# An expert loop over turns of four tiles, written out on three engines

## The chip, the cores and the metric

The kernel runs on one core of one Trainium2 chip. The metric is device time in microseconds (us), the median of several executions; a profiled execution of the same program gives the trace. Five engines work side by side, each with its own stream of instructions and its own sequencer: PE (TensorE, matrix products), ACT (ScalarE), DVE (VectorE), POOL (GpSimd) and SP (SyncE, which here only issues DMAs). They meet only through semaphores.

## The reference, cut to what matters

One layer over 32 x 64 tokens of width 256: attention over itself and over a context, and behind it a mixture of experts with a dense shared branch. The part around the change is the routed one:

```python
E, TOPK, INTER = 8, 2, 512
logits = x @ router_w
top_logits, top_indices = jax.lax.top_k(logits, TOPK)
scores = jax.nn.softmax(top_logits, axis=-1)
sorted_pos = jnp.argsort(top_indices.reshape(-1), stable=True)
permuted = x[sorted_pos // TOPK]
expert_ids = top_indices.reshape(-1)[sorted_pos]
for e in range(E):
    mask = (expert_ids == e)[:, None]
    g, u = jnp.split(permuted * mask @ w1[e], 2, axis=-1)
    out = out + jnp.where(mask, silu(g) * u @ w2[e], 0.0)
# each token: its two rows, weighted by its scores, plus the shared branch
```

## The kernel before

Everything is on one core and in one program: first the attention (up to about 690 us), then the shared branch with the routing beside it, and from about 813 us the routed experts, in a block of its own. Only that last block is touched.

The routed rows, 2 x 2048 of them, were sorted by expert and scattered to a buffer in HBM, each expert's rows padded to whole tiles of 128. There are ET = 39 tiles (line 42). A tile belongs to one expert, which is known only when the kernel runs. The weights of all eight experts lie in SBUF as two 16-bit parts each (`w1h`, `w1l`, `w2h`, `w2l`), so that an expert's weights are read at an address that a register holds.

The tiles are taken in turns of TURN = 4 (line 43). For each turn one word of `ecode` holds the numbers of six experts as digits to the base 8: those of its own four tiles and of the two after. `experts(q, count)` (line 1611 on) reads that word on PE with a value load (line 1613) and splits it into registers (line 1617). This stands at the head of each turn.

One slot, for tile t, holds on PE, in this order (`turn`, line 1621 on):

- `first(t + 2)`: 12 products of the gate and up projection into `b_eg` and `b_eu` (line 1588), which wait for `gl` of that tile from DVE and for the `ea` of the tile before
- `gather_T(t + 3)`: 4 transposes of the tile's rows into `b_x` (line 1578)
- `second(t)`: 12 products of the down projection into `b_ey` (line 1606)
- `product_T(t + 1)`: 8 transposes of the activation into `b_a` (line 1598)

ACT and DVE have slots of their own, in step with this: ACT `gate` (line 1654, `esg`), `high` (line 1650, `gh`), `split` (line 1660, `eah`), `output` (line 1669, into the tile's own row in `xg`) and `high_T` (line 1665, `aTh`); DVE `product` (line 1707, `ea`), `low` (lines 1700 and 1701, `gl` and `uys`), `split` (line 1712, `eal`) and `low_T` (line 1717, `aTl`). The two parts of a number, high and low, make the products exact enough in 16 bits.

POOL adds each finished tile to `out` in HBM with an indirect DMA that accumulates (line 1567); it waits for ACT's `output` of that tile and for the landing of the DMA before it. POOL's 39 steps are written out already. SP loads the tiles of the later turns in eight DMAs in a loop of its own (line 1554 on) and one more behind it.

ET = 39 gives NQT = 9 whole turns and a rest of three tiles. Turn 0 is written out, since its rows lie in another tile (`xhl`). Turns 1 to 8 are one body in a hardware loop, in which `t` is computed from the loop's register: on PE in line 1641, on ACT and DVE in `slots` (line 1535 on, the loop in line 1539). The rest is written out again.

Of the kernel before, what the change touches and what calls it, by code (L numbers as in the profile page):

```python
# [41 lines left out]
ET = (2 * T + E * (P - 1)) // P  # L42
TURN = 4
# [22 lines left out]
def build(nc, x, ctxT, cols, w_all, wprojT,  # L66
# [4 lines left out]
    with ExitStack() as top:  # L71
# [69 lines left out]
        def after(eng, name, count):  # L141

            if not (isinstance(count, int) and count <= 0):
                eng.wait_ge(s[name], count)
# [919 lines left out]
        with ExitStack() as ph:  # L1064
# [94 lines left out]
            @block.sync  # L1159
            def _(sp):  # L1160
                attention_sync(sp)
                sp.wait_ge(s["proj_done"], 4 * (4 * NT - 2))
                for n in range(NPC):
                    if n == 2:
                        sp.wait_ge(s["wsq_done"], NPC)
                    after(sp, "wl_done", n - 2)
                    sp.dma_start(stage[n % 3][:, :], ffw[n, :, :]).then_inc(s[f"wst_in{n % 3}"], 16)
                    if n == 4:
                        store_rows(sp, NT - 2)
                    if n == 6:  # L1170
                        store_rows(sp, NT - 1)
                        sp.wait_ge(s["row_out"], 16 * NT)
                        sp.wait_ge(s["proj_done"], 16 * NT)
                        sp.dma_start(xn[:, :, 0:2 * H].bitcast(U32), rowbuf).then_inc(s["rows_in"], 16)
                sp.wait_ge(s["scattered"], 16 * 2 * NT)
                sp.wait_ge(s["gu_done"], NS)
                sp.dma_start(xg0.bitcast(U32), x_rows[:, 0:TURN, :])\
                    .then_inc(s["xg_in"], 16)
                sp.wait_ge(s["xg_in"], 16)
# [335 lines left out]
        with ExitStack() as ph:  # L1515
            NQT = ET // TURN
# [19 lines left out]
            def slots(eng, slot):  # L1536
                for t in range(TURN):
                    slot(t, t % 2)
                with eng.Fori(1, NQT) as q:
                    for n in range(TURN):  # L1540
                        slot(TURN * q + n, n % 2)
                for t in range(NQT * TURN, ET):
                    slot(t, t % 2)

            def xrow(t):
                return row(xg0, t) if isinstance(t, int) and t < TURN else row(xg, t - TURN)

            def exists(t):
                return not isinstance(t, int) or t < ET
# [21 lines left out]
            @block.tensor  # L1571
            def _(pe):
                def gather_T(t, n, m):
                    if m == 0:
                        pe.wait_ge(s["xg_in"], 16 * (t // TURN + 1) if isinstance(t, int) else 16 // TURN * t + 16)
                    after(pe, "gl_done", t)
                    for k in range(2 * KT):
                        last = pe.transpose(b_x[:, 0, k * P:(k + 1) * P], xrow(t)[:, k * P:(k + 1) * P], ident16[:, :])  # L1578
                    last.then_inc(s["gT_done"], 1)

                def first(t, n, e):
                    pe.wait_ge(s["gl_done"], t + 1)
                    after(pe, "ea_done", t - 1)
                    for k in range(KT):
                        for m, (xx, w) in enumerate(((gh, w1h), (gh, w1l), (gl, w1h))):
                            for c, o in enumerate((b_g[n], b_u[n])):
                                at = k * 2 * F + c * F
                                last = pe.matmul(o[:, :], xx[n][:, k * P:(k + 1) * P],  # L1588
                                                 w[:, bass.ds(e, 1), at:at + F].rearrange("p a b -> p (a b)"),
                                                 start=(k == 0 and m == 0), stop=(k == KT - 1 and m == 2))  # L1590
                    last.then_inc(s["eh_done"], 1)

                def product_T(t, n):
                    pe.wait_ge(s["eal_done"], t + 1)
                    after(pe, "aTl_done", t)
                    for m, a in enumerate((ah, al)):
                        for c in range(FK):
                            last = pe.transpose(b_a[:, m, c * P:(c + 1) * P], a[n][:, c * P:(c + 1) * P], ident16[:, :])  # L1598
                    last.then_inc(s["aT_done"], 1)

                def second(t, n, e):
                    pe.wait_ge(s["aTl_done"], t + 1)
                    after(pe, "ysb_done", t)
                    for c in range(FK):
                        for m, (a, w) in enumerate(((aTh, w2h), (aTh, w2l), (aTl, w2h))):
                            last = pe.matmul(b_y[:, 0:H], a[n][:, c * P:(c + 1) * P],  # L1606
                                             w[:, bass.ds(e, 1), c * H:(c + 1) * H].rearrange("p a b -> p (a b)"),
                                             start=(c == 0 and m == 0), stop=(c == FK - 1 and m == 2))
                    last.then_inc(s["ey_done"], 1)

                def experts(q, count):

                    code = pe.value_load(ecode[0:1, bass.ds(q, 1)], min_val=0, max_val=E ** CODE - 1)
                    held = []
                    for n in range(count):
                        reg = pe.alloc_register()
                        pe.reg_mov(reg, code // E ** n % E)
                        held.append(bass.RuntimeValue.of_register_unchecked(reg, min_val=0, max_val=E - 1))
                    return held

                def turn(q, t0, slots):
                    es = experts(q, min(slots + 2, ET - t0) if isinstance(t0, int) else CODE)
                    for n in range(slots):
                        t = t0 + n
                        if exists(t + 2) and exists(t + 3):
                            first(t + 2, n % 2, es[n + 2])
                            gather_T(t + 3, (n + 1) % 2, (n + 3) % TURN)
                        second(t, n % 2, es[n])
                        if exists(t + 1):
                            product_T(t + 1, (n + 1) % 2)  # L1630
                        if exists(t + 2) and not exists(t + 3):
                            first(t + 2, n % 2, es[n + 2])

                for t in range(3):
                    gather_T(t, t % 2, t)
                es = experts(0, 2)
                first(0, 0, es[0])
                first(1, 1, es[1])
                product_T(0, 0)
                turn(0, 0, TURN)  # L1640
                with pe.Fori(1, NQT) as q:
                    turn(q, TURN * q, TURN)
                turn(NQT, NQT * TURN, REST)

            @block.scalar
            def _(act):
# [34 lines left out]
                def slot(t, n):  # L1681
# [7 lines left out]
                    if exists(t + 2) and not exists(t + 3):  # L1689
                        gate(t + 2, n)  # L1690
                        split(t + 2, n)

                slots(act, slot)

            @block.vector
# [98 lines left out]
```

## Time and profile before

| | |
|---|---|
| median of 3 runs | 1024.51 us (1024.0 to 1026.1) |
| the profiled execution | 1024.13 us |
| its span in the trace | 1022.0 us |
| mean granted clock of PE over the span | 0.986 of full speed |
| PE busy | 955.7 us, 94% of the span |
| DVE busy | 797.4 us, 78% |
| ACT busy | 735.2 us, 72% |
| POOL busy | 452.4 us, 44% |
| the routed stage, turns 1 to 8 on PE | 841.44 to about 1000 us |

All times in the trace are counted from the span's start. The span is what the engines' records cover; the time of the execution is a little longer. PEld is PE's loading of weights, which runs beside its products.
### The profile page before, as it was taken

The numbers are of one execution on the slowest core, as the hardware profiler recorded it, in microseconds if no ns is written. First come the engines' busy times: TensorE is split into PE (matmuls) and PEld (weight loads), VectorE is DVE, ScalarE is ACT, GpSimd is POOL, SyncE is SP. The second block draws the span as 40 slices with busy tenths as digits, with TensorE's granted clock in tenths as the row PEclk, the third lists the DMA queues.
The fourth block names the chain that finished last, engine by engine and source line by source line (L and its number), as shares of the span: only waits on it lengthen the run. The fifth ranks groups of instructions, "written<-read, shape, count | busy, mean of one in ns | idle before, by whom it ended". The sixth has DMA issues, their size and how long they took to land. (4 is left out here: it accounts for less than half of the span.)

```text
span 1022.0 us, 22255 instructions
## 1 busy us (share of the span) xinstructions
PE 955.7 (94%) x7240; PEld 677.0 (66%) x7241; DVE 797.4 (78%) x1704; ACT 735.2 (72%) x1364; POOL 452.4 (44%) x673
## 2 busy tenths in 40 slices
PE   5588999999999999999999999989999799999994
PEld 3356677777777777777777777756556456666663
DVE  7678999999999999999999999886997444444441
ACT  6868898898898898898898898753655354454552
POOL 5224556455455455455455455501066113333332
PEclk9899999999999999999999999999999999999997
DMA  9923311011011011001011011315266553222222
GB/s 266 252 77 63 62 36 34 27 34 36 27 34 35 28 32 38 27 31 38 27 32 37 28 31 38 109 47 171 86 207 191 185 147 69 26 30 27 26 26 26
DMA packets 37100, 70.16 MB, mean 69 GB/s; under 512 B 3984, under 2 KB 25104, under 8 KB 36880
## 3 DMA queue, kind: packets, MB, share of 16 engines
q1 hardware_dynamic: 27552, 54.39, 17.3%
q0 software_dynamic: 9456, 14.59, 8.4%
q8 instruction: 52, 0.85, 0.3%
q14 instruction: 40, 0.33, 0.1%
HBM read 55.52 MB, written 18.68 MB: 73 GB/s over the span
## 5 line engine op out<-in xcount | busy, mean ns | idle before, releaser
L664 POOL TENSOR_TENSOR root<-vareps,neghalf 128x4 f32<-128x4 f32 (+1 forms) x128 | 174.4, 1362 | 10.0
L657 POOL TENSOR_TENSOR var<-ssq,unit 128x4 f32<-128x4 f32 (+1 forms) x128 | 53.1, 415 | 252.0 <-DVE ssq L496 252.0
L329 PE MATMUL b_pj<-w_hi,xq 128*128 128x512 f16 x384 | 147.7, 385 | 1.8 <-DVE xq L647 1.5
L329 PE MATMUL b_pj<-w_lo,xq 128*128 128x512 f16 x384 | 146.9, 382 | 0.0
L430 ACT ACTIVATE sq<-b_pj 128x512 f32<-128x512 f32 x192 | 114.3, 595 | 44.2 <-PE b_pj L329 41.5
L496 DVE TENSOR_REDUCE ssq<-sq 128x4 f32<-128x512 f32 x192 | 130.1, 677 | 11.9 <-ACT sq L430 11.9
L507 DVE TENSOR_TENSOR nrm<-raw,rstd 128x512 f32<-128x512 f32 x192 | 128.1, 668 | 1.1 <-POOL rstd L668 0.8
L355 PEld LDWEIGHTS b_sc<-kT,qT 128*128 128x128 f32 x1024 | 122.4, 192 | 5.0 <-ACT qT L456 0.3
L355 PE MATMUL b_sc<-kT,qT 128*128 128x64 f32 x1024 | 122.8, 273 | 0.0
L345 PE MATMUL b_tr<-ident,nrm 128*128 128x128 f32 x768 | 117.1, 275 | 5.3 <-DVE nrm L507 5.1
L440 ACT ACTIVATE raw<-b_pj 128x512 f32<-128x512 f32 x192 | 115.8, 603 | 0.0
L345 PEld LDWEIGHTS b_tr<-ident,nrm 128*128 128x128 f32 x768 | 94.0, 146 | 31.7 <-DVE nrm L507 8.0
L1567 POOL DMA_INDIRECT out<-xg x35 | 54.3, 1551 | 114.9 <-ACT xg L1669 90.8
L456 ACT ACTIVATE qT<-b_tr,col 128x512 f32<-128x512 f32 x128 | 99.8, 780 | 4.0 <-PE b_tr L345 4.0
L1707 DVE SCALAR_TENSOR_TENSOR ea<-b_eu,uu,esg 128x512 f32<-128x512 f32 x39 | 29.3, 751 | 88.6 <-ACT esg L1654 88.6
L545 DVE TENSOR_TENSOR cat<-b_o,rsm 128x512 bf16<-128x512 f32 x128 | 81.8, 680 | 4.2 <-PE b_o L382 4.2
L1654 ACT ACTIVATE esg<-b_eg,ug 128x512 f32<-128x512 f32 x39 | 26.8, 687 | 74.8 <-PE b_eu L1588 74.8
L382 PE MATMUL b_o<-probT,v 64*128 64x128 f32 x1024 | 74.4, 285 | 0.0
L382 PEld LDWEIGHTS b_o<-probT,v 64*128 64x128 f32 x1024 | 62.1, 187 | 11.5 <-issue 11.5
L456 ACT ACTIVATE kT<-b_tr,col 128x512 f32<-128x512 f32 x64 | 49.5, 773 | 25.0 <-PE b_tr L345 25.0
L419 PE MATMUL b_acc<-wproj,catq 128*128 128x256 f16 x512 | 66.3, 272 | 0.0
L329 PEld LDWEIGHTS b_pj<-w_hi,xq 128*128 128x128 f16 x384 | 37.7, 98 | 33.1 <-DVE xq L647 1.8
(312 smaller groups left out, 2316.3 us busy)
## 6 DMA issues: line engine op xcount, KB each, us to landing
nst<-in_ffw SPq DMA_DIRECT2D x40, 512.0 KB, 3.6
wload<-in_ffw SPq DMA_DIRECT2D x20, 512.0 KB, 3.9
xbuf<-zero SPq DMA_DIRECT2D x39, 129.0 KB, 4.0
xg<-xbuf SPq DMA_DIRECT2D x8, 516.0 KB
x_sb<-in_x SPq DMA_DIRECT2D x4, 512.0 KB, 13.0
wproj<-in_ctxT SPq DMA_DIRECT2D x1, 2048.0 KB, 9.7
xhl<-in_w_all SPq DMA_DIRECT2D x4, 512.0 KB, 20.3
wproj<-in_wprojT POOLq DMA_DIRECT2D x4, 512.0 KB, 6.1
```

Source lines behind the costliest of these rows:

```text
L329: last = pe.matmul(o, x, w[kind][:, k, at:at + BANK], start=(k == 0 and n_ == 0), stop=(k == KT - 1 and n_ == len(terms) - 1))
L345: last = pe.transpose(o, nrm[:, c, hd * P:(hd + 1) * P], ident[:, :])
L355: last = pe.matmul(b_sc[:, (g * 2 + b) * S:(g * 2 + b + 1) * S], qT[:, r % 2, g * 2 + b, :], kT[:, r % 2, g, b * S:(b + 1) * S], start=Tru ...
L382: last = pe.matmul(b_o[b][:, g * P:(g + 1) * P], v[b * S:(b + 1) * S, r, g, :], probT[b * S:(b + 1) * S, r % 2, g, :], start=True, stop=True)
L419: last = pe.matmul(b_acc[:, 0:H], catq[:, r % 2, hd, :], wproj[:, r * n + hd, :], start=(r == 0 and hd == 0), stop=(r == 3 and hd == n - 1))
L430: act.activation(sq[:, (r * NN + c) % 2, :], b_pj[c % 2][:, :], ACT.Square).then_inc(s["sq_done"], 1)
L440: act.activation(raw[:, r % 2, c, :], bk, ACT.Copy).then_inc(s["raw_done"], 1)
L456: act.activation(flat(dst), b_tr[:, :], ACT.Identity, scale=col[:, at:at + 1], bias=col[:, at + 1:at + 2]).then_inc(s["tev_done"], 1)
L496: dve.tensor_reduce(ssq[:, r % 2, c, :], sq[:, (r * NN + c) % 2, :].rearrange("p (a b) -> p a b", b=D), axis=AX.X, op=ALU.add).then_inc(s[ ...
L507: dve.tensor_tensor(nrm[:, c, :].rearrange("p (a b) -> p a b", b=D), raw[:, r % 2, c, :].rearrange("p (a b) -> p a b", b=D), wide(rstd[:, ...
L545: last = dve.tensor_tensor(cat16[:, :, b * S:(b + 1) * S], b_o[b][:, :].rearrange("p (a b) -> p a b", b=S), wide(rsm[:, r * n:(r + 1) * n] ...
L664: pool.tensor_tensor(root[:, r % 2, c, :], vareps[:, r % 2, c, :], neghalf[:, 0:1].unsqueeze(2).to_broadcast(shape), ALU.pow).then_inc(s[" ...
```

## The change

The hardware loop over turns 1 to 8 is replaced by a loop of the program's builder, which writes the eight bodies out one after the other. This is done for PE and, in `slots`, for ACT and DVE. The work, its order on each engine and the waits between engines stay. `t` and `q` are then constants: addresses and the values waited for are too, apart from the expert's number, which is read as before from `ecode` at the head of each turn. SP's loop and POOL's stream are left as they are.

```diff
@@ -1536,10 +1536,7 @@
             def slots(eng, slot):
                 for t in range(TURN):
                     slot(t, t % 2)
-                with eng.Fori(1, NQT) as q:
-                    for n in range(TURN):
-                        slot(TURN * q + n, n % 2)
-                for t in range(NQT * TURN, ET):
+                for t in range(TURN, ET):
                     slot(t, t % 2)
 
             def xrow(t):
@@ -1638,7 +1635,7 @@
                 first(1, 1, es[1])
                 product_T(0, 0)
                 turn(0, 0, TURN)
-                with pe.Fori(1, NQT) as q:
+                for q in range(1, NQT):
                     turn(q, TURN * q, TURN)
                 turn(NQT, NQT * TURN, REST)
```

## Rows read from the trace of the kernel before

**Rows 1.** Page, part 2: PE's busy share in 40 slices of the span, in tenths

```profile
PE   5588999999999999999999999989999799999994
```

**Rows 2.** Waits, 790 to 1022 us: who waited for whom, us in total, times, longest

```profile
PE b_eg L1588 <- issue: 6.2, 9, 1.5
...
PE b_eg L1588 <- DVE gl L1700: 1.4, 8, 0.2
```

**Rows 3.** Timeline of PE, a slot's first product: start, duration, idle before in brackets

```profile
831.80 0.39 PE L1588 MATMUL b_eg<-w1h,gh 128*128 x1
...
836.41 0.39 PE L1588 MATMUL b_eg<-w1h,gh 128*128 x1
...
841.44 0.39 PE L1588 MATMUL b_eg<-w1h,gh 128*128 x1 [0.28 <-issue]
...
871.10 0.39 PE L1588 MATMUL b_eg<-w1h,gh 128*128 x1
...
875.89 0.39 PE L1588 MATMUL b_eg<-w1h,gh 128*128 x1
...
980.62 0.39 PE L1588 MATMUL b_eg<-w1h,gh 128*128 x1 [0.60 <-issue]
...
995.13 0.39 PE L1588 MATMUL b_eg<-w1h,gh 128*128 x1
```

**Rows 4.** Timeline of all engines, a slot of turn 0, written out

```profile
834.19 0.38 PE L1588 MATMUL b_eu<-w1h,gl 128*128 x1
834.60 0.69 ACT L1654 ACTIVATE esg<-b_eg,ug 128x512 f32<-128x512 f32 x1 [1.62 <-PE b_eu L1588]
...
835.32 0.75 DVE L1707 SCALAR_TENSOR_TENSOR ea<-b_eu,uu,esg 128x512 f32<-128x512 f32 x1 [1.89 <-ACT esg L1654]
835.99 0.28 DVE L1700 COPY gl<-b_x 128x256 f16<-128x256 f16 x1
```

**Rows 5.** The same in the loop; last, ACT's register operation, from line 1654's instructions

```profile
873.48 0.38 PE L1588 MATMUL b_eu<-w1h,gl 128*128 x1
874.00 0.69 ACT L1654 ACTIVATE esg<-b_eg,ug 128x512 f32<-128x512 f32 x1 [1.72 <-PE b_eu L1588]
...
874.80 0.75 DVE L1707 SCALAR_TENSOR_TENSOR ea<-b_eu,uu,esg 128x512 f32<-128x512 f32 x1 [2.08 <-ACT esg L1654]
875.47 0.28 DVE L1700 COPY gl<-b_x 128x256 f16<-128x256 f16 x1
...
L1654 ACTq FUSED_REGOPS  x1: 43/43/43, 873.9 to 873.9; - x1
```

**Rows 6.** Instructions of lines 1641, 1613: ns min/median/max, first and last start us

```profile
L1641 PEldq COMPARE_BRANCH  x8: 79/218/245, 859.1 to 998.3; - x8
L1641 PEldq MOVE  x1: 37/37/37, 839.5 to 839.5; - x1
...
L1613 PEldq TENSOR_LOAD <-ecode x1: 315/315/315, 839.7 to 839.7; - x1
```

**Rows 7.** Timeline of ACT (the output of tile 4), then of POOL's scatters

```profile
846.70 0.46 ACT L1669 ACTIVATE xg<-b_ey,uys 128x256 f32 x1
...
850.18 1.55 POOL L1567 DMA_INDIRECT out<-xg  x1 [3.24 <-DMA out<-xhl]
...
881.92 1.55 POOL L1567 DMA_INDIRECT out<-xg  x1 [3.09 <-ACT xg L1669]
...
1000.89 1.56 POOL L1567 DMA_INDIRECT out<-xg  x1 [3.23 <-ACT xg L1669]
...
1010.09 1.55 POOL L1567 DMA_INDIRECT out<-xg  x1 [3.08 <-DMA out<-xg]
...
1014.57 1.55 POOL L1567 DMA_INDIRECT out<-xg  x1 [2.93 <-ACT xg L1669]
```

**Rows 8.** DMA queue of instruction fetches, 100 to 700 and 815 to 850 us: packets, MB, share

```profile
q8 instruction: 39, 0.64, 0.4%
...
q8 instruction: 3, 0.05, 0.6%
```

## Prediction, made before the changed kernel was seen

> **What bounds the kernel now.** I read the page first: PE is busy for 94% of the span, and at nine tenths or more in most of its 40 slices [rows 1], so only idle time of PE, or what makes PE late, is worth anything. The change touches only the routed stage, from about 813 us to the end. There I read who waited for whom [rows 2]: PE stands idle ahead of the first gate product `b_eg` for two reasons, 6.2 us in 9 places named "issue" (PE's own sequencer is not ready) and 1.4 us in 8 places on DVE's `gl`. These sums miss short gaps, because a matmul record is longer than the distance to the next. So the view to trust is the timeline: the starts of the first `b_eg` product of each slot [rows 3]. A slot that is written out (turn 0) lasts 836.41 - 831.80 = 4.61 us. The same slot inside the loop lasts 875.89 - 871.10 = 4.79 us, with the same 36 matmuls. The loop thus costs 0.18 us in every slot, besides what the turn's edge costs.
>
> **Where the 0.18 us comes from.** I follow the one ring that runs through three engines: last product of `first` on PE, then `gate` on ACT, `product` and `low` on DVE, then the next `first` on PE. Written out [rows 4, 3]: 834.19 to 834.60 (0.41), to 835.32 (0.72), to 835.99 (0.67), to the next `b_eg` at 836.41 (0.42), 2.22 us. In the loop [rows 5, 3]: 873.48 to 874.00 (0.52), to 874.80 (0.80), to 875.47 (0.67), to 875.89 (0.42), 2.41 us. The two links that are longer are those in which ACT and DVE must compute an address between the wait and the operation: ACT's register operation of 43 ns with its gap [rows 5] costs 0.10 us, DVE's likewise 0.09 us. Written out, `t` is a constant and neither exists. PE is then at its own pace, since in turn 0 the last transpose and the next `first` are almost back to back.
>
> **The change part by part, against the profiled execution's own time (span 1022.0 us, 1024.13 us with what lies around it).**
>
> 1. The loop's own instructions on PE. A back edge has an addition, a branch (218 ns median) and one register operation before the code is loaded [rows 6]; with their gaps that is about 0.50 us (0.03 + 0.22 + 0.05 and three gaps of 0.06, the gap being what MOVE at 839.5 and the load at 839.7 leave beside 37 and 50 ns). There are seven taken branches, one entry (about 0.20 us) and one exit. The head of each turn stays: value load, the range check and the digits. It can't be hidden, since `first` needs its digits and PE's queue runs dry.
>
> 2. What a written-out turn will last. The slot from 836.41 to 841.44 is the nearest row [rows 3]: its four stages are written out, and at its end stands a head with the entry's 0.20 us in it. Less that, a slot with a head is 5.03 - 0.20 = 4.83 us. A turn is then 3 x 4.61 + 4.83 = 18.66 us. Before, seven turns from head to head lasted 980.62 - 841.44 = 139.18 us, 19.88 each.
>
> 3. The sum on PE. At the first head 0.20. Over the seven turns 139.18 - 7 x 18.66 = 8.56. The last three slots of the loop, from 980.62 to 995.13 [rows 3], are 14.51 us and become 13.83: 0.68. Behind the loop the path goes once more through ACT and DVE before PE can go on, which gives another 0.19 by the links above; the exit branch lies beside that and gives nothing. Sum 9.6 us. The last tile would be ready that much earlier, and its scatter could start at 1014.57 - 9.6 = 1005.0 [rows 7], where it is released by ACT.
>
> 4. What is late next: POOL. It adds one tile at a time to `out` and waits for each landing before the next issue. At tile 4 it is behind: ACT has written that tile by 846.70 + 0.46, but its scatter starts only at 850.18, released by the DMA before it [rows 7]. That start hangs on landings that are slow while the big loads run, and none of them moves. From there seven cycles bound by landings last 881.92 - 850.18 = 31.74 us, and two more near the end 1010.09 - 1000.89 = 9.20: mean 4.55 us. Now the slots are longer (19.88 / 4 = 4.97 us) and POOL catches up by tile 11. After the change they average 18.66 / 4 = 4.67, only 0.12 us more than POOL's cycle, so its lag of some 3 us takes about 26 tiles to close. Scatter-bound all the way, tile 38 would start at 850.18 + 34 x 4.55 = 1004.9. So both chains arrive within 0.1 us of each other, and the end follows the later of the two, each with its own scatter. I add 0.2 us for that: 1005.2, a gain of 9.4 us. Nothing waits for POOL but the end, since the rows of `xg` are not used again.
>
> 5. Code that is written out must be fetched. Queue q8 moves it in packets of 16 KB. The trace can't show what a fetch costs in turns 1 to 8, for there the loop fetches none. In the attention stage 39 packets came in 600 us, and their time is 0.4% of 16 engines, 0.98 us each [rows 8], while PE was at nine tenths or more in each of those slices [rows 1]. In the written-out part of the routed stage 3 packets came in 35 us [rows 8], and the slots of 4.61 us are timed in just that part. At this rate the new turns need some 12 more. The bounds are 0 (all ahead of need) and 12 x 0.98 = 11.8 us (PE waits for each in full). I take 0, by the nearest row, which is the same code written out.
>
> The Trainium skill, "Runtime: NRT & Kernel Launch", section "Instruction fetch mechanics", says that crossing a 16 KiB block is mostly hidden and that a taken branch to a page no longer held stalls. The second would make the back edge dearer than I reckon; here it does not show, as the branches took 0.08 to 0.25 us [rows 6]. The first agrees with turn 0.
>
> 6. ACT's and DVE's own loop instructions go too. They lie beside PE's work except for the two links counted above: nothing more. SP's loop of loads is not touched.
>
> **The rivals.**
>
> - The scatter chain is slower than its mean. It is bound by landings at every tile, and other traffic (the fetches among it) may lengthen each. Against it: nine cycles average 4.55. With 4.64 throughout, tile 38 starts at 850.18 + 34 x 4.64 = 1007.9, a gain of 6.7: 1017.8 us. This takes over as soon as a cycle exceeds 4.56.
> - Only the branches are saved, and the 0.18 us per slot stays (because, say, the addresses of the routed expert, which stay in registers, set the slot). For it: PE keeps its register operations for the weights. Against it: turn 0 has these too and runs at 4.61. Then 7 x 0.50 + 0.20, and 0.2 for the exit, 3.9 us: 1020.6 us.
> - The other side: PE waits for its code. Mechanism: each of 12 new 16 KB packets on q8 arrives late. Price up to 0.98 us each; 11.8 us against 9.4 gained is 2.4 us slower, 1026.9 us. It decides from 9.4 / 12 = 0.78 us per packet. Against it: turn 0 and the attention stage. Half that stall would give 1021.
> - The change doesn't reach the chip's time, because the instructions that remain refill the space: no change, 1024.5 us.
>
> **How the numbers follow.** The median of the runs is 1024.51, 0.38 above the profiled execution. Forecast: 1024.13 - 9.4 + 0.4 = 1015.1 us. Chances: forecast as summed, 0.66; slower scatter chain, 0.14; only the branches, 0.07; some stalls for code but still a gain, 0.04; PE waits for its code and the kernel is slower, 0.06; no change, 0.03. The range takes in the first two: the low end is the sum with every head at its shortest and POOL always in time (9.6 and 0.1 less at each of eight heads, 10.4), 1014.1, put at 1014.0; the high end is the slow scatter chain, 1018.0. That holds 0.80. A measurement of this kernel can tell about 0.2% (2 us) from no change; so faster 0.91, within 0.03, slower 0.06.
>
> **What would show it.** Right: every slot without a head at 4.61 us from one `b_eg` to the next, slots with a head at 4.83; no branch and no register operation of ACT or DVE between turns; idle time on `gl` gone while "issue" before `b_eg` stays, smaller; POOL released by its own DMA up to the last third of the stage, at 4.5 to 4.6 us per tile; about 12 more packets on q8. Wrong: slots of 4.79 (second rival), idle time of PE in places that are no heads (third), or a last scatter that starts later than 1006 and is released by a DMA (first).

## The result, and the profile after

| | before | after |
|---|---|---|
| median | 1024.26 us (4 runs, 1023.8 to 1026.1) | 1015.91 us (4 runs, 1014.6 to 1016.7) |
| the profiled execution | 1024.13 | 1016.18 |
| its span | 1022.0 | 1014.5 |
| first `b_eg` of turn 0's last slot (tile 5) | 836.41 | 838.11 |
| first `b_eg` of tile 37 | 995.13 | 987.33 |
| start of the last scatter | 1014.57 | 1007.05 |
| instructions in the trace | 22255 | 21771 |

The ratio of the times is 0.9914, with a 95% interval from 0.9897 to 0.9931: 8.4 us faster by the medians, where 9.4 was forecast. Measured twice more beside before, the same kernel gave 0.9936 (0.991 to 0.9962) and 0.9926 (0.9911 to 0.994).

First the waits in the profile after, 790 to 1015 us (who waited for whom, us in total, times, longest):

```profile
POOL out L1564 <- DMA out<-xg: 74.8, 24, 4.1
...
POOL out L1564 <- ACT xg L1666: 30.1, 10, 3.1
...
PE b_eg L1585 <- issue: 1.5, 2, 1.3
```

Against [rows 2], PE's idle time named "issue" ahead of `b_eg` fell from 6.2 to 1.5 us, and the line on `gl` is gone. The view names POOL's own DMA 24 times; the same row of before, at the tiles in `xg`, was

```profile
POOL out L1567 <- DMA out<-xg: 20.9, 7, 3.1
```

The timeline of PE after, at the starts of slots (the first product of `first`; line 1585 is 1588 of before):

```profile
838.11 0.39 PE L1585 MATMUL b_eg<-w1h,gh 128*128 x1
...
842.90 0.39 PE L1585 MATMUL b_eg<-w1h,gh 128*128 x1
...
861.52 0.39 PE L1585 MATMUL b_eg<-w1h,gh 128*128 x1
...
866.13 0.39 PE L1585 MATMUL b_eg<-w1h,gh 128*128 x1
...
870.74 0.39 PE L1585 MATMUL b_eg<-w1h,gh 128*128 x1
...
987.33 0.39 PE L1585 MATMUL b_eg<-w1h,gh 128*128 x1
```

The slot after a head is now 866.13 - 861.52 = 4.61 us, a plain one the same, and one with a head 842.90 - 838.11 = 4.79, against 4.79 and 5.03 in [rows 3]. The ring that [rows 5] showed in the loop, from the trace after:

```profile
868.51 0.38 PE L1585 MATMUL b_eu<-w1h,gl 128*128 x1
868.93 0.69 ACT L1651 ACTIVATE esg<-b_eg,ug 128x512 f32<-128x512 f32 x1 [1.63 <-PE b_eu L1585]
...
869.65 0.75 DVE L1704 SCALAR_TENSOR_TENSOR ea<-b_eu,uu,esg 128x512 f32<-128x512 f32 x1 [1.89 <-ACT esg L1651]
870.32 0.28 DVE L1697 COPY gl<-b_x 128x256 f16<-128x256 f16 x1
```

Its links are 0.42, 0.72 and 0.67 us, and 0.42 to PE at 870.74: those of [rows 4] within a hundredth. At POOL (timeline, with the output of the last tile on ACT put last):

```profile
849.44 1.55 POOL L1564 DMA_INDIRECT out<-xg  x1 [3.00 <-DMA out<-xhl]
...
886.14 1.55 POOL L1564 DMA_INDIRECT out<-xg  x1 [2.99 <-ACT xg L1666]
891.72 1.55 POOL L1564 DMA_INDIRECT out<-xg  x1 [4.03 <-DMA out<-xg]
...
1007.05 1.55 POOL L1564 DMA_INDIRECT out<-xg  x1 [2.97 <-ACT xg L1666]
...
1005.90 0.47 ACT L1666 ACTIVATE xg<-b_ey,uys 128x256 f32<-128x256 f32 x1 [3.38 <-PE b_ey L1603]
```

The last scatter starts 1007.05 - 1005.90 = 1.15 us behind the start of ACT's output. Where a scatter waits for ACT alone that distance is 0.73 to 0.75 us; at the last tile of before it was 0.80. So some 0.35 us of the gain went to the landings.

The names in the waits hide how tight this chain is. In the profile after, every one of the 34 scatters from tile 5 to 38 starts 0.77 us after the landing of the one before, also the ten that the view puts down to ACT: POOL never caught up. In before only ten of the 34 do so, tiles 5 to 11 and the last three. Tiles 36 and 37 are bound by landings in every trace with all scatters, and tile 38 in all but pe_alone and act_dve, since ACT's output of tile 36 comes only 3.1 us behind that of tile 35.

Queue q8 moved 11 packets of code from 850 to 990 us:

```profile
q8 instruction: 11, 0.18, 0.6%
```

### The profile page after: what moved, and what is told of

The parts are those of the page before. It is cut to its first block and busy times, and to the rows that moved or that the text cites. A ratio compares the mean times of both kernels' runs of the same rounds, so it can differ in the third digit from the quotient of the medians.

```text
span 1014.5 us, 21771 instructions
## 1 busy us (share of the span) xinstructions
PE 952.3 (94%) x7240; PEld 676.3 (67%) x7240; DVE 797.7 (79%) x1704; ACT 735.2 (72%) x1364; POOL 448.5 (44%) x673
```

## The experiments

Absolute times differ between executions by a microsecond or two before the changed code is reached, so two distances within a trace are compared: from the first `b_eg` of turn 0's last slot to that of tile 37 (PE's pace), and from the same point to the last scatter. A "slot with a head" is the one at whose end the turn's code is read.

| kernel | time, us (runs), beside before | to tile 37 | to last scatter | slots: plain (median), after a head, with a head |
|---|---|---|---|---|
| before | 1024.3 to 1025.5, medians | 158.72 | 178.16 | 4.80, 4.92, 5.29 to 5.52 |
| after | 1015.91 (4), 1024.26 | 149.22 | 168.94 | 4.61, 4.61, 4.78 to 4.99 |
| after2 | 1016.99 (5), 1025.50 | 149.38 | 168.65 | 4.61, 4.61, 4.82 to 4.88 |
| after3 | 1016.05 (6), 1024.82 | 149.42 | 168.83 | 4.61, 4.61, 4.78 to 5.04 |
| pe_alone | 1022.39 (10), 1025.50 | 155.63 | 175.06 | 4.80, 4.92, 4.80 to 5.07 |
| act_dve | 1019.30 (4), 1025.50 | 153.00 | 172.24 | 4.61, 4.61, 5.08 to 5.38 |
| act_alone | 1022.94 (1), 1024.74 | 156.07 | 175.47 | 4.70, 4.81, 5.02 to 5.39 |
| dve_alone | 1021.22 (1), 1024.74 | 155.45 | 174.76 | 4.71, 4.72, 5.11 to 5.39 |
| few_scatters | 1015.33 (1), 1024.74 | 151.16 | 170.40 | 4.61, 4.61, 4.86 to 5.14 |
| pe_few | 1020.64 (1), 1024.74 | 154.67 | 174.74 | 4.80, 4.92, 4.80 to 4.81 |
| early_codes | 1013.96 (4), 1025.50 | 147.64 | 167.73 | 4.61, 4.61, 4.61 |
| early_codes2 | 1014.51 (4), 1024.82 | 147.59 | 172.10 | 4.61, 4.61, 4.61 |
| early_few | 1010.90 (1), 1024.82 | 147.52 | 166.75 | 4.61, 4.61, 4.61 to 4.65 |
| loop_early | 1013.45 (4), 1024.86 | 148.65 | 168.02 | 4.61, 4.61, 4.74 to 4.76 |

### Which engine's loop costs what

`pe_alone` undoes the change on ACT and DVE, `act_dve` undoes it on PE:

```diff
# pe_alone, against before
-                with pe.Fori(1, NQT) as q:
+                for q in range(1, NQT):
# act_dve, against after
-                for q in range(1, NQT):
+                with pe.Fori(1, NQT) as q:
```

> Only PE's turns are written out; ACT and DVE keep their loop. Theory (the slot is set by the ring through ACT and DVE, the head by PE): slots in the loop's part stay at 4.80 us, the one after a head at 4.92, slots with a head fall from 5.3 to about 4.83; 7 x 0.5 + 0.2 + 0.2 = 3.9 us less than before: about 1020.4 us. Rival (PE's own register operations for addresses and waits set the slot): slots fall to 4.61, and the time to that of the changed kernel, 1015 to 1016 us.

> Only ACT and DVE are written out; PE keeps its loop. Theory: slots fall to 4.61 us, also the one after a head; slots with a head stay at about 5.3; per turn 19.88 becomes 13.83 + 5.32 = 19.15, so 7 x 0.73 + 0.68 + 0.19 = 6.0 us less: about 1018.3 us. With the run in which PE alone is written out the two gains add up to 9.6 to 9.9. Rival (PE's register operations): slots stay at 4.79 and nothing is gained, 1024 us.

Timelines of PE in pe_alone:

```profile
866.59 0.39 PE L1588 MATMUL b_eg<-w1h,gh 128*128 x1 [0.18 <-DVE gl L1700]
871.39 0.39 PE L1588 MATMUL b_eg<-w1h,gh 128*128 x1
...
876.19 0.39 PE L1588 MATMUL b_eg<-w1h,gh 128*128 x1
...
881.26 0.39 PE L1588 MATMUL b_eg<-w1h,gh 128*128 x1 [0.29 <-issue]
```

and in act_dve:

```profile
870.13 0.39 PE L1585 MATMUL b_eg<-w1h,gh 128*128 x1
...
874.74 0.39 PE L1585 MATMUL b_eg<-w1h,gh 128*128 x1
...
880.04 0.39 PE L1585 MATMUL b_eg<-w1h,gh 128*128 x1 [0.55 <-issue]
```

Written out on PE alone, the plain slot stays at 4.80 us and the idle time on `gl` stays. Written out on ACT and DVE alone it is 4.61, while PE still runs its loop. So the rival that put the 0.18 us on PE's own register operations is out. The distance to tile 37 falls by 3.09 and 5.72 us; together 8.81, where the whole change gives 9.50. By the medians the two gave 3.1 and 6.2 us, where 3.9 and 6.0 were expected. Most of what pe_alone lacks shows in its slots with a head: some are 4.80 us, four are 5.04 to 5.07, a matter that comes up again below.

`act_alone` and `dve_alone` give `slots` a second form and use it on one engine:

```diff
-            def slots(eng, slot):
+            def slots(eng, slot, written=False):
+                if written:
+                    for t in range(ET):
+                        slot(t, t % 2)
+                    return
...
-                slots(act, slot)
+                slots(act, slot, True)
```

(for `dve_alone` the last line is that of DVE).

> Only ACT's turns are written out; PE and DVE keep the loop. Theory (each link of the ring carries its own engine's register operation): plain slots in the loop's part fall from 4.80 to 4.70 us, the one after a head from 4.92 to about 4.81, slots with a head stay at about 5.3 to 5.4. Rival (one engine alone carries the whole 0.18): 4.61 or 4.80. From turn 0's last slot to the slot of tile 37 that is some 2.5 to 3.2 us less than the 158.7 us of before.

> Only DVE's turns are written out. Theory: plain slots 4.71 us (0.09 less), the one after a head about 4.72 (its second register operation of 0.12 us goes too), slots with a head 5.3 to 5.4; the stretch to tile 37 some 2.8 to 3.5 us shorter than the 158.7 us of before. With ACT alone the plain slots' gains add up to 0.18 to 0.19. Rival (one engine carries it all): 4.61 or 4.80.

The same view of act_alone, then of dve_alone:

```profile
872.08 0.39 PE L1592 MATMUL b_eg<-w1h,gh 128*128 x1
...
876.78 0.39 PE L1592 MATMUL b_eg<-w1h,gh 128*128 x1
```

```profile
871.40 0.39 PE L1592 MATMUL b_eg<-w1h,gh 128*128 x1
...
876.11 0.39 PE L1592 MATMUL b_eg<-w1h,gh 128*128 x1
```

Plain slots of 4.70 and 4.71 us, 0.10 and 0.09 off, which add up to the 0.19 (one execution each, but the slots repeat to 0.01 us within it). The slot after a head is 4.81 and 4.72: the 0.12 us more that it took in the loop belong to DVE. Each link of the ring carries its own engine's register operation, as expected.

### A value load and a scatter at the same moment

The long heads of pe_alone have long value loads. Line 1613's loads there (ns min/median/max), then one of them with the scatter ahead of it:

```profile
L1613 PEldq TENSOR_LOAD <-ecode x8: 302/547/578, 859.9 to 996.2; - x8
```

```profile
877.15 1.55 POOL L1567 DMA_INDIRECT out<-xg  x1 [3.25 <-ACT xg L1669]
...
L1613 PEldq TENSOR_LOAD <-ecode x1: 542/542/542, 879.3 to 879.3; - x1
```

The load began 2.1 us after the scatter's start. Two kernels leave scatters out: `few_scatters` is the changed kernel without those of odd tiles from 5 to 37, `pe_few` is pe_alone without those of tiles 2, 6, 10 up to 34, the ones that preceded the heads; their output lacks these tiles.

```diff
# few_scatters
-                for t in range(ET):
+                left = [t for t in range(ET) if t < 5 or t == ET - 1 or t % 2 == 0]
+                for n, t in enumerate(left):
                     pool.wait_ge(s["ysb_done"], t + 1)
-                    after(pool, "y_out", 16 * t)
+                    after(pool, "y_out", 16 * n)
# pe_few
+                left = [t for t in range(ET) if t % TURN != 2 or t == ET - 1]
```

> The changed kernel without the scatter to the output of every odd tile from tile 5 to 37; these tiles' part is left out of the output, all else is computed. PE's slots as in the changed kernel, so the stretch from turn 0's last slot to that of tile 37 stays at 149.2 to 149.4 us. Theory (the last scatter was 0.05 to 0.4 us late, by the landing before it): the last scatter starts 0.73 to 0.80 us behind ACT's last output, and the stretch from turn 0's last slot to the last scatter is 168.4 to 168.7 us against 168.95 and 168.65: level with PE, worth at most half a microsecond. Rival (the scatter chain sets the pace of the stage): over 1.5 us less.

> The kernel in which PE alone is written out, without the scatter of tiles 6, 10, ... 34 and tile 2 (every fourth, whose part is left out of the output). Those are the tiles whose scatter started 2.0 to 2.2 us before a head's value load, and just these loads took 0.50 to 0.58 us instead of 0.30, in five of eight heads, which made the head's slot 5.04 to 5.07 instead of 4.80 us. Theory (the load is slowed by the scatter that moves the rows at the same moment): all loads of the heads take 0.30 to 0.33 us and no slot with a head is over 4.85 us; the stretch from turn 0's last slot to that of tile 37 falls from 155.6 to about 154.4 us. Rival (the code's place in the written-out stream makes some loads slow): the same heads, at 879, 899, 938, 957 us, stay at 0.54 us.

The heads' loads in pe_few, then in few_scatters:

```profile
L1614 PEldq TENSOR_LOAD <-ecode x8: 297/302/306, 859.6 to 994.9; - x8
```

```profile
L1611 PEldq TENSOR_LOAD <-ecode x8: 547/562/576, 858.9 to 991.4; - x8
```

In pe_few every load takes 0.30 us, every slot with a head 4.80 or 4.81, and the distance to tile 37 falls by 0.96 us though nothing on PE has changed. That is the effect expected, at the heads named. The expectation for few_scatters failed, and this is worth more: with half the scatters gone, PE became slower (151.16 instead of 149.22 us). The kept scatters no longer queue behind each other; each starts as soon as ACT is done, and so those of tiles 6, 10, ... 34 now start 2.1 us ahead of a head's load. All eight loads take 0.55 to 0.58 us, and the slots with these heads 5.06 to 5.14. In the changed kernel POOL's lag of 1 to 2 us keeps most loads out of that window.

Over 14 traces (108 value loads behind 850 us), all 20 loads of 0.44 us or more began 1.96 to 2.30 us after the start of a scatter; none of the other 88 took over 0.38. What they share at that moment is not shown. The scatter's first packets begin 2.12 us after its start in every trace, and the load reads SBUF, as they do; but they go on to about 3.4 us, and loads that began at 2.33 to 2.63 us took only 0.30 to 0.36. So it is the packets' beginning that coincides with the long loads, not their whole time.

few_scatters was also meant to show whether the last scatter is held back. In it the last one starts 0.75 us behind ACT's output (1006.85 to 1007.60), against 1.15 in the changed kernel; but its PE was slower, so its end says nothing on the sum.

### Codes read early: is the scatter chain now the bound?

`early_codes` loads the next turn's code behind slot 0 and splits it behind slots 1 and 2, where PE's sequencer stands waiting; turn 0's code is read together with the first.

```diff
+                        if count and n == 0:
+                            code = load(q + 1)
+                        if count and n == 1:
+                            following += digits(code, 0, min(3, count))
+                        if count and n == 2:
+                            following += digits(code, 3, count)
...
-                es = experts(0, 2)
+                es = digits(load(0), 0, CODE)
```

> The changed kernel with each turn's code loaded and split during the turn before (load in slot 0, three digits each in slots 1 and 2), where PE's sequencer stands waiting for about 1.4 us. Both theories: no slot above 4.66 us, PE ready 8 x 0.185 + 0.28 = 1.8 us earlier. My theory (the scatter chain, 4.55 to 4.65 us per tile, is level with PE already): the last scatter starts at most 0.6 us earlier and is released by a DMA; every scatter from tile 4 on is released by the landing before it; the time is within 0.6 us of the changed kernel's in the same rounds. Rival (PE still sets the end): the time falls by the whole 1.5 to 1.8 us.

The slots with a head become 4.61 us. By the medians the time fell by 3.0 us (from 1016.99 in after2, two of whose five executions were above 1020), not by 0.6 at most, so my expectation was wrong and the rival's was too low. The step that failed was turn 0's head: I had put it at 0.28 us, but the slot it stands in fell from 4.89 to 3.58, by 1.31. Not all of that is gained, since six digits instead of two are now split ahead of the first product: from turn 0's value load to that product it took 2.47 us instead of 1.87 to 1.95. From that value load to the last scatter, which leaves out the spread ahead of the stage, the trace gives 191.55 us against 193.52 to 193.88 in the three of the changed kernel: 2.0 to 2.3 us. And with everything ahead of tile 4 earlier, the scatter chain, which I had taken as fixed there, started earlier too in this execution. Of the rest, 149.22 - 147.64 = 1.58 us, the end received 168.94 - 167.73 = 1.21. At its end the chain holds (POOL, and ACT's last output):

```profile
1002.82 0.47 ACT L1674 ACTIVATE xg<-b_ey,uys 128x256 f32<-128x256 f32 x1 [3.38 <-PE b_ey L1603]
1004.42 1.55 POOL L1564 DMA_INDIRECT out<-xg  x1 [3.07 <-DMA out<-xg]
```

1.60 us instead of 0.75: 0.85 held back. `early_few` is early_codes with the scatters of few_scatters (its output lacks the same tiles).

> The early codes without the scatter of every odd tile from 5 to 37 (left out of the output). Theory (with the codes out of the way the scatter chain is the bound by 0.8 us at the end): PE's slots are unchanged, 147.6 us from turn 0's last slot to that of tile 37, though the value loads may take 0.55 us; the last scatter starts 0.75 to 0.8 us behind ACT's output instead of 1.6, and the stretch from turn 0's last slot to it falls from 167.7 to about 166.9 us. Rival (the load in slot 0 would delay the next slot when it is slow): slots of tile 6, 10, ... over 4.7 us and the stretch to tile 37 over 148.5.

```profile
1002.37 0.47 ACT L1675 ACTIVATE xg<-b_ey,uys 128x256 f32<-128x256 f32 x1 [3.33 <-PE b_ey L1604]
1003.12 1.55 POOL L1565 DMA_INDIRECT out<-xg  x1 [8.98 <-ACT xg L1675]
```

PE's pace is the same (147.52), the last scatter follows ACT by 0.75 us, and the distance to it is 166.75, as expected. So with PE at 4.61 us per slot the chain of scatters is a second bound, by somewhat under a microsecond in that execution.

### The spread, and what a fetch of code does to a scatter

> The changed kernel once more, for its spread. My theory: in every profile the stretch from turn 0's last `b_eg` slot (838.11 us in the first profile) to the last scatter is 168.9 us against 178.2 us before, whatever the absolute times are; the 1.2 us by which the changed kernel's attention stage came later begin in the first 75 us, where the code is the same, and are scatter between executions, so that they need not return. Rival: the longer program costs about 1.2 us ahead of the routed stage each time; then the stage begins again at 815 rather than 813.7 us and the median stays at 1015.9. Theory: some profile shows the stage beginning at 813.7 to 814.5, and medians between 1014.8 and 1016. Also: if a landing is slowed by a fetch of code at the same moment (two of 34 landings took 4.8 and 4.9 us and lay beside packets of q8), the slow landings lie beside q8 packets again; if not, they lie anywhere.

> The changed kernel a third time, in five rounds, because single executions of it spread from 1014.6 to 1022.5 us while 14 of before lay within 1024.8 to 1025.9. Theory (its phase against the scatters varies: POOL lies 1 to 2 us behind ACT, and where it catches up, the scatter meets the heads' value loads, each 0.25 us dearer, up to 8 x 0.25 = 2 us): most executions at 1014.6 to 1017, the profile's heads at 4.79 to 4.88 us where POOL lags by over 1 us and the load takes 0.30, and 5.0 or more only where the load starts 2.0 to 2.2 us behind a scatter. Rival (code fetches stall PE in some executions): slots without a head over 4.7 us. The median 8 to 9.5 us under before.

> The kernel with the codes read a turn earlier, again, beside the changed kernel on the same chip. Theory: 1.3 us from turn 0's head, which no products cover, and 1.6 us from the eight heads after it, less 0.4 to 0.9 us that the scatter chain holds back at the end: 2 to 3 us under the changed kernel's median, and a narrower spread, since its loads lie where PE's sequencer waits anyway and a slow load costs nothing. Rival (the 3.0 us of the first comparison came from two slow executions of the changed kernel): less than 1.5 us.

The stage began at 814.65 us in after2, between the 813.73 of before and the 815.09 of the first profile of after, which decides nothing; but it began at 814.40 in after3, and at 813.35 in few_scatters, which differs from after only in its scatters. So the 1.4 us were scatter between executions, as expected. Over all 14 traces it lay between 813.35 and 815.34. But the changed kernel spreads more at the top: its 15 executions run from 1014.6 to 1022.5 us, four of them above 1019, while the 25 of before measured beside after2 and after3 lay between 1024.39 and 1025.88. The expected cause, long loads worth 2 us at most, is too small for that.

The expectation for early_codes2 failed in its size: it was 1016.05 - 1014.51 = 1.5 us under the changed kernel's median, where 2 to 3 were expected. That is nearly the rival's figure, so the 3.0 us of the first time may come in part from two long executions of the changed kernel. It spread by 3.3 us, against 4.5 in after3: less, but not little.

The profile of early_codes2 happened to be such an execution (1017.01 us, its others 1013.7 to 1014.9). PE's pace is unchanged to 0.05 us. What differs is POOL:

```profile
842.97 1.55 POOL L1564 DMA_INDIRECT out<-xhl  x1 [3.26 <-DMA out<-xhl]
849.77 1.55 POOL L1564 DMA_INDIRECT out<-xg  x1 [5.25 <-DMA out<-xhl]
...
895.32 1.55 POOL L1564 DMA_INDIRECT out<-xg  x1 [3.07 <-DMA out<-xg]
901.14 1.73 POOL L1564 DMA_INDIRECT out<-xg  x1 [4.28 <-ACT xg L1674]
...
933.47 1.71 POOL L1564 DMA_INDIRECT out<-xg  x1 [2.90 <-ACT xg L1674]
939.78 1.55 POOL L1564 DMA_INDIRECT out<-xg  x1 [4.60 <-DMA out<-xg]
...
1007.99 1.55 POOL L1564 DMA_INDIRECT out<-xg  x1 [2.88 <-DMA out<-xg]
```

Three scatters took 6.80, 5.82 and 6.31 us to the next instead of 4.55. At a slot of 4.61 POOL gains back only 0.06 us per tile, so the lag stayed: ACT's last output began at 1001.94, the scatter 6.05 us later. The three delays, 2.25, 1.27 and 1.76 us, add up to the 5.3 us by which that is more than 0.75. Before the change a slot was 4.97 us on the mean, 0.42 above the chain's cycle, and a lag of 6 us would be gone after some 14 tiles.

The last two of the three lie beside a packet on q8 (the first falls into the time of the big loads). They are no exception: over 11 traces with all scatters, 363 landings of tiles 5 to 37, ten took more than 4.3 us, and each had a packet of code on q8 that began 1.8 to 3.0 us after the scatter's start. The 341 landings without a packet at 1.4 to 3.1 us took 3.79 us on the mean and 4.07 at most; the 22 with one took 4.40 on the mean. In the five of these traces in which PE keeps its loop, and q8 brings at most two packets from 850 to 990 us, none of 165 landings was above 4.07.

PE hardly waited for its code: with all three engines written out no slot without a head was above 4.68 us in any trace. Slots of 4.65 to 4.68 instead of 4.61 occur at most twice in a trace, and only where PE is written out; that a fetch causes them is not shown.

For the changed kernel's own executions above 1019 us the cause is argued, since none of them was profiled. They are 4 to 7 us longer than the shortest, which would take several such landings, or a late start at tile 4 besides. Their mean granted clocks (0.982, 0.982, 0.984 and 0.984) lie at or just under those of the others (0.984 to 0.987), so a part by the clock is not ruled out.

`loop_early` draws both conclusions. ACT and DVE are written out, PE keeps the loop and so fetches nothing, and the code is read early:

```diff
+                def own(n):
+                    reg = pe.alloc_register()
+                    pe.reg_mov(reg, held[n])
+                    return bass.RuntimeValue.of_register_unchecked(reg, min_val=0, max_val=E - 1)
...
+                        if ahead and n == 0:
+                            code = load(q + 1)
+                        if ahead and n > 0:
+                            digits(code, *((), (0, 1), (2, 4), (3, 5))[n])
...
                with pe.Fori(1, NQT) as q:
                    turn(q, TURN * q, TURN)
```

> PE keeps its hardware loop, ACT and DVE are written out, and each turn's code is loaded in slot 0 of the turn before and split in its slots 1 to 3 (digits 3 and 5 behind the last slot, since their registers are in use until then). Theory (what costs is what stands between PE's last transpose and the next first product, not the loop itself): at a turn's edge only addition, branch, one register operation and two digits are left, some 0.9 us, which start 3.06 us into a slot of 4.61 and so are hidden; all slots 4.61 to 4.66 us, 147.6 us from turn 0's last slot to that of tile 37, as in the kernel with early codes written out. PE fetches no code in turns 1 to 8 (2 or 3 packets of q8 in 850 to 990 us, not 11), so no landing after tile 4 takes over 5 us beside one: time 1013.5 to 1014.5 us, or 10 to 11.5 us under before, with less spread. Rival (a taken branch on PE is exposed in any case): slots with a head of 5.1 us, about 1017.

PE's slots around a turn's edge, and the instruction queues from 850 to 990 us, among which q8 has no row:

```profile
873.82 0.39 PE L1585 MATMUL b_eg<-w1h,gh 128*128 x1
...
878.57 0.39 PE L1585 MATMUL b_eg<-w1h,gh 128*128 x1
...
883.18 0.39 PE L1585 MATMUL b_eg<-w1h,gh 128*128 x1
```

```profile
q1 hardware_dynamic: 400, 0.40, 1.0%
q14 instruction: 5, 0.04, 0.1%
```

The edge costs 4.75 - 4.61 = 0.14 us, neither hidden in full, as I had expected, nor the 0.5 of the rival; to tile 37 it is 148.65 us where 147.6 were expected. No landing took over 3.90 us. Its four executions lay within 1013.2 to 1013.85 us, median 1013.45, ratio 0.9889 (0.9873 to 0.9906). early_codes has the same ratio, 0.9889 (0.9872 to 0.9905), and 0.9896 (0.9881 to 0.991) the second time: the two can't be told apart. So writing PE's turns out was not needed for the gain.

Its end shows the second bound once more (POOL, and ACT's last output):

```profile
1002.53 0.47 ACT L1677 ACTIVATE xg<-b_ey,uys 128x256 f32<-128x256 f32 x1 [2.12 <-PE b_ey L1603]
1004.67 1.55 POOL L1564 DMA_INDIRECT out<-xg  x1 [3.08 <-DMA out<-xg]
```

The scatter of tile 35 was in time, 0.73 us behind ACT, but the last one starts 2.14 us behind: the three cycles to it took 13.79 us, PE and ACT only 12.38. In before the last scatters took 13.68 and ACT 13.61, level. ACT is earlier here because the last tile's down products ran at a granted clock of 1.00, the level of 2.4 GHz (1001.0 to 1002.5 us), while it was 0.50, that of 1.2 GHz, in before (1011.1 to 1013.7) and in after (1003.1 to 1005.8). PE's idle times just ahead, 1.6 and 1.2 us, are the same in all three; why the clock differs is open. Nothing was gained by it, since the landings set the end.

## Why the prediction was right

- **The slot (0.18 us).** Right. Read from the written-out turn 0, it came out at 4.61, and the links at the values of [rows 4]. pe_alone, act_dve, act_alone and dve_alone show it belongs to ACT (0.10) and DVE (0.09).
- **The head.** A slot with a head was put at 4.83 us; it was 4.79 in most turns and 4.99 in one with a load of 0.50 us. A load of 532 ns stood in the trace of before, among seven in the loop, the others near 0.30; I had not looked at what set it. That the head "can't be hidden" holds for the order of this kernel alone: in early_codes it costs no slot anything.
- **The sum on PE.** 0.20 + 8.56 + 0.68 = 9.44 us to tile 37 were forecast, 158.72 - 149.22 = 9.50 measured. The 0.19 behind it shrank to 0.07: from tile 37 to ACT's last output 18.64 became 18.57.
- **The scatter chain, level with PE.** It came out level, 0.35 us late where 0.2 was allowed, but in part by luck. The cycle from tile 4 on was (1007.05 - 849.44) / 34 = 4.64 us, not 4.55, which costs 3.1 us over 34 tiles; two landings of 4.8 and 4.9 us, both beside packets of q8, make 2 us of that. That is the first rival's cycle. The start at tile 4, which I had taken as fixed, made up for it: counted from the first `b_eg` of tile 5 it came at 849.44 - 838.11 = 11.33 us instead of 850.18 - 836.41 = 13.77, 2.4 earlier, since the landings before it happened to be short. In the traces it lay anywhere from 847 to 851 us. With the start of before and the measured cycle the gain would have been the rival's 6.7.
- **Code fetches.** 12 packets were forecast, 11 came between 850 and 990. The cost on PE, taken as 0, was at most two slots of 0.05 to 0.07 us in a trace. One reading behind it was a little off: [rows 1] have eight tenths, not nine, in one slice of the attention stage (664 to 690 us). That fetches lengthen a landing was named under the first rival as a possibility ("the fetches among it") and left out of the sum; beside them stand two of the three delays, 3.0 of 5.3 us, in the one long execution that was profiled.
- **From the stage to the whole.** In the profiled execution the stage gave 178.16 - 168.94 = 9.22 us. Of that, 838.11 - 836.41 = 1.70 us was taken back because that execution came late to tile 5. Outside the span the time fell from 2.1 to 1.7 us. Net 7.95. The medians give 8.4.
- **The rivals.** "Only the branches" and "PE waits for its code" are out. The first one, the slower chain, put at 1017.8 us, had the cycle right (4.64 us); its time was missed only because the chain started earlier. That it also made the executions above 1017 us is argued.

## What to carry to other kernels

In a ring of engines that hand a tile around, the register operation that an engine needs between its wait and its operation is on the path; look for it on the engines that are not busy, and write the loop out there first. Move what the sequencer must compute for the next turn to where it stands waiting, and a hardware loop costs little (0.14 us per turn in loop_early). When one bound is brought down to within a per cent of a second one (here 4.61 us per slot against a chain of 4.55 per landing), delays that used to be made up stay until the end; the spread of the times grew here, and the one long execution that was profiled shows this as its cause.

## What the runs showed of the hardware

- A value load on PE's sequencer takes 0.30 us, but 0.44 to 0.58 us when it begins 1.96 to 2.30 us after the start of an accumulating scatter of a tile (20 of 20 such long loads; no load that began at another moment took over 0.38). Taking the scatters ahead of it away brings it back to 0.30.
- A packet of 16 KB of code that is fetched 1.8 to 3.0 us after such a scatter's start can lengthen its landing from 3.8 us to between 4.4 and 5.5; it was so for ten of the 22 packets at 1.4 to 3.1 us.
- A scatter on POOL that waits for the landing of the one before starts 0.77 us after that landing; one that waits for ACT's output alone starts 0.27 us after its end.
- The time outside the span was 2.0 to 2.1 us for the kernels in which DVE keeps its loop and 1.7 to 1.8 us for those in which it is written out. The reason stays open.
